# Groups of x: who centres and rounds them ahead of the transposes, and in which slot

## What is computed

```python
def _layernorm(x, axis=-1, eps=1e-05):
    m = jnp.mean(x, axis=axis, keepdims=True)
    v = jnp.var(x, axis=axis, keepdims=True)
    return (x - m) / jnp.sqrt(v + eps)

def _act_quant(x):
    scale = 127.0 / jnp.clip(jnp.max(jnp.abs(x), axis=-1, keepdims=True), 1e-05)
    xq = jnp.clip(jnp.round(x * scale), -128.0, 127.0) / scale
    return x + jax.lax.stop_gradient(xq - x)

x = x + jnp.tanh(g_xattn[0]) * _L0_xattn_ref(_layernorm(x), ctx_1024, ctx_1024, ...)
x = x + jnp.tanh(g_ffn[0]) * _L0_ffn_ref(_layernorm(x), w_gate, w_up, w_down)

gate = jax.nn.silu(_bitlinear(x, w_gate)); up = _bitlinear(x, w_up)
return _bitlinear(gate * up, w_down)        # each _bitlinear quantises its input with _act_quant
```

## Time and profile before

| | |
|---|---|
| median of three runs | 793.21 us (792.26 to 796.49) |
| the profiled execution | 792.8 us, of it the span from first to last instruction 791.0 us |
| busy share of the span | PE 89%, DVE 90%, ACT 86%, Pool 62% |
| slots 258 to 283 (groups 0 to 11) | about 641 to 688 us |
| tiles from s = 0 on | about 688 to 791 us |

### The profile page before, as it was taken

How to read it: one execution, slowest core, us unless ns; L and a number is a source line. 1 busy time by engine, 2 the same in 40 slices (tenths; PEclk the granted TensorE clock), 3 DMA queues, 4 the chain that set the end, 5 groups by cost and what they waited for, 6 DMA issues and landing times.

```text
span 791.0 us, 20866 instructions
## 1 busy us (share of the span) xinstructions
PE 702.7 (89%) x7118; PEld 474.6 (60%) x7127; DVE 708.0 (90%) x1452; ACT 683.9 (86%) x1454; POOL 487.9 (62%) x956
## 2 busy tenths in 40 slices
PE   6567899999999999999999999999999888877896
PEld 4334566666666666667676766676765555533453
DVE  5779899989899999999999999899999776798995
ACT  1578899898999999999999999999999888768883
POOL 4747657667777667676766666767664043245663
PEclk9666899999999999999999999999999899999998
DMA  9997747464668575767455666656664122246688
GB/s 206 204 261 166 197 127 149 109 126 128 154 120 149 124 144 124 145 122 158 123 138 134 134 137 133 128 136 130 124 118 85 39 68 86 71 103 164 160 179 181
DMA packets 148887, 108.50 MB, mean 137 GB/s; under 512 B 56991, under 2 KB 145183, under 8 KB 148767
## 3 DMA queue, kind: packets, MB, share of 16 engines
q1 hardware_dynamic: 143630, 101.98, 58.3%
q10 hardware_dynamic: 5152, 5.19, 2.7%
HBM read 49.54 MB, written 12.85 MB: 79 GB/s over the span
## 4 chain that ended last, share of the span: by engine, by line
PE 36%; ACT 35%; DVE 16%; issue 9%; DMA 2%; ACTq 1%; POOL 1%; SPq 0%; DVEq 0%; POOLq 0%
ACT ex L1197 13%; ACT pt L1187 12%; PE p_o L1348 7%; PE p_m L1426 6%; PE p_s L1328 5%; PE p_m L1407 5%; PE p_t L1369 4%; DVE kst L1032 3%; DVE hmax L1035 3%; PE p_m L1415 3%; ACT L1223 3%; ACT L1187 2%; DVE stats L907 2%; PE p_m L1399 2%; DVE nm L926 2%
## 5 line engine op out<-in xcount | busy, mean ns | idle before, releaser
L1197 ACT ACTIVATE ex<-p_s,nm 112x375 f32<-112x375 f32 x512 | 275.8, 618 | 12.3 <-DVE nm L926 11.0
L1187 ACT ACTIVATE pt<-p_t,ct 128x336 f32<-128x336 f32 x488 | 245.8, 577 | 26.7 <-PE p_t L1369 24.5
L907 DVE BATCH_NORM_STATS2 stats<-ex 112x6 f32<-112x375 f32 x512 | 252.5, 535 | 1.4 <-ACT ex L1197 1.3
L926 DVE TENSOR_REDUCE nm<-p_s 112x2 f32<-112x750 f32 x256 | 236.0, 922 | 1.2 <-PE p_s L1328 1.0
L1328 PE MATMUL p_s<-kst,qst 96*112 96x375 bf16 x512 | 154.8, 348 | 13.5 <-ACT ex L1197 7.3
L1369 PE MATMUL p_t<-qst,kst 99*128 99x112 bf16 x1464 | 115.1, 213 | 4.9 <-ACT pt L1187 4.0
L1369 PEld LDWEIGHTS p_t<-qst,kst 99*128 99x128 bf16 x1464 | 91.1, 98 | 44.0 <-issue 19.7
L1407 PE MATMUL p_m<-wv_sb,ctxt 128*128 128x256 f32 (+1 forms) x384 | 106.7, 401 | 4.7 <-DVE va L859 2.9
L1348 PE MATMUL p_o<-pt,va 128*32 128x112 f32 (+1 forms) x3072 | 101.7, 265 | 1.4 <-ACT pt L1187 0.8
L1426 PE MATMUL p_m<-ctxt,wk_sb 128*128 128x375 f32 x240 | 94.6, 518 | 1.7 <-DVE qf L875 1.1
L1328 PEld LDWEIGHTS p_s<-kst,qst 96*112 96x112 bf16 x512 | 67.0, 139 | 45.7 <-ACT ex L1197 34.6
(11 more groups left out here) (187 smaller groups left out, 1164.3 us busy)
## 6 DMA issues: line engine op xcount, KB each, us to landing
kst<-kp SPq DMA_DIRECT2D x378, 93.8 KB, 3.5
ctxt<-ctxt_dram SPq DMA_DIRECT2D x32, 375.0 KB, 4.2
qbounce<-qp SPq DMA_DIRECT2D x32, 168.0 KB, 2.5
qst<-qbounce SPq DMA_DIRECT2D x32, 168.0 KB, 3.6
qst<-qbounce SPq DMA_DIRECT2D x32, 112.0 KB, 3.4
xm<-x_dram SPq DMA_DIRECT2D x32, 112.0 KB, 2.4
x_dram<-x SPq DMA_DIRECT2D x32, 112.0 KB, 1.9
xt<-x_dram SPq DMA_DIRECT2D x28, 128.0 KB, 3.2
```

The source lines that it names most:

```text
L907: last = nc.vector.bn_stats(stats[:, nb % RING, 2 * pb + i], ex[0:SQ, 2 * (t % 2) + i, :])
L926: nc.vector.tensor_reduce(nm[:, n % RING, 2 * p:2 * p + 2], p_s[t % 2][0:SQ, :, 0:SK], axis=AX.X, op=ALU.max, negate=True).then_inc(s_max, 1)
L1187: nc.scalar.activation(pt[:, (2 * r + i) % 8], st_home(r, i)[:, 0:KC * SQ].rearrange("k (c q) -> k c q", c=KC), ACT.Exp, scale=ct[:, nr % ...
L1197: nc.scalar.activation(ex[0:SQ, 2 * ((t - 1) % 2) + i, :], p_s[(t - 1) % 2][0:SQ, i, 0:SK], ACT.Exp, bias=nm[:, ne % RING, h:h + 1]).then_ ...
```

## The change

Pool centres the groups and rounds them; ACT's `round_group` is gone, and with it the column of zeros. At slot 258 + 2i Pool negates the means of group i into `xneg` (the tile of the inverses, under another name), adds them to x in two instructions and signals `s_cen`. DVE takes maximum, scale and inverse one slot later, at 259 + 2i. Pool's `quant_group` stays at 260 + 2i and now first multiplies by the inverse and adds ROUND, in two instructions; in Pool's queue it stands ahead of the centring of the next group in the same slot. Loads wait for `s_cen` of the group two before. For groups 12 and 13 all steps behind the centring are a tile later; for groups 0 to 11 transposes and copies stay in their slots. The diff, without the counts of semaphores that follow from it:

```diff
@@ def load_group(i) (SyncE) @@
                 if i >= 2:
-                    sp.wait_ge(s_gx, count(4, i - 2, 1))
+                    sp.wait_ge(s_cen, count(1, i - 2, 1))
@@ slot(t) (Pool) @@
                 i = group_at(t, 2)
                 if i is not None:
                     quant_group(i)
+                i = group_at(t, 0)
+                if i is not None:
+                    centre_group(i)
+
+            def centre_group(i):
+
+                of = slice(GROUP * i, GROUP * (i + 1))
+                pool.wait_ge(s_ag, GROUP * (i + 1))
+                nc.gpsimd.tensor_scalar(xneg[:, of], mv2[:, of, 0], -1.0, 0.0, ALU.mult, ALU.add).then_inc(s_neg, 1)
+                pool.wait_ge(s_gl[i % 2], ring_count(16 * GROUP, i, 2))
+                if i == 0:
+                    pool.wait_ge(s_bn, SLOTS * B)
+                if i >= 2:
+                    pool.wait_ge(s_gq, count(1, i - 2, 1))
+                pool.wait_ge(s_neg, count(1, i, 1))
+                for g in range(GROUP):
+                    k = GROUP * i + g
+                    last = nc.gpsimd.tensor_scalar(fxn[:, i % 2, g], xl[:, i % 2, g], xneg[:, k:k + 1], 1.0, ALU.add, ALU.mult)
+                last.then_inc(s_cen, 1)
 
             def quant_group(i):
 
+                pool.wait_ge(s_gx, count(3, i, 3))
+                for g in range(GROUP):
+                    k = GROUP * i + g
+                    last = nc.gpsimd.tensor_scalar(fxn[:, i % 2, g], fxn[:, i % 2, g], xinv[:, k:k + 1], ROUND, ALU.mult, ALU.add)
+                last.then_inc(s_gr, 1)
                 pool.wait_ge(s_gr, count(1, i, 1))
@@ tile(s) (Pool) @@
-                if s - 2 in LATE_AT:
-                    quant_group(LATE_AT[s - 2])
+                if s - 3 in LATE_AT:
+                    quant_group(LATE_AT[s - 3])
+                if s in LATE_AT:
+                    centre_group(LATE_AT[s])
@@ slot(t) (DVE) @@
-                i = group_at(t, 0)
+                i = group_at(t, 1)
                 if i is not None:
                     x_group(i)
@@ x_group(i) (DVE) @@
-                dve.wait_ge(s_gl[i % 2], ring_count(16 * GROUP, i, 2))
-                dve.wait_ge(s_ag, GROUP * (i + 1))
-                if i == 0:
-                    dve.wait_ge(s_bn, SLOTS * B)
-                if i == TAILED:
-                    dve.wait_ge(s_e2, 2 * SLOTS * B)
-                    nc.vector.memset(zero, 0.0).then_inc(s_zero, 1)
-                    dve.wait_ge(s_zero, 1)
-                if i >= 2:
-                    dve.wait_ge(s_gq, count(1, i - 2, 1))
-                for g in range(GROUP):
-                    k = GROUP * i + g
-                    if i < TAILED:
-                        last = nc.vector.tensor_scalar(fxn[:, i % 2, g], xl[:, i % 2, g], mv2[:, k, 0:1], None, ALU.subtract)
-                    else:
-                        last = nc.vector.scalar_tensor_tensor(out=fxn[:, i % 2, g], in0=xl[:, i % 2, g], scalar=mv2[:, k, 0:1],
-                                                              in1=zero.to_broadcast([P, D]), op0=ALU.subtract, op1=ALU.add)
-                last.then_inc(s_gx, 1)
-                dve.wait_ge(s_gx, count(4, i, 1))
+                dve.wait_ge(s_cen, count(1, i, 1))
                 nc.vector.tensor_reduce(xmax[:, of], fxn[:, i % 2], axis=AX.X, op=ALU.max, apply_absolute_value=True).then_inc(s_gx, 1)
@@ slot(t) and tile(s) (ACT) @@
-                i = group_at(t, 1)
-                if i is not None:
-                    round_group(i)
-
-            def round_group(i):
-
-                act.wait_ge(s_gx, count(4, i, 4))
-                for g in range(GROUP):
-                    k = GROUP * i + g
-                    last = nc.scalar.activation(fxn[:, i % 2, g], fxn[:, i % 2, g], ACT.Copy, scale=xinv[:, k:k + 1], bias=ROUND)
-                last.then_inc(s_gr, 1)
```

More of the change, by code:

```diff
@@ L144, in gated_block @@
         xmax, xsc, xinv = sb("xmax", [P, TILES]), sb("xsc", [P, TILES]), sb("xinv", [P, TILES])
+        xneg = xinv
         gsc, usc = sb("gsc", [P, TILES]), sb("usc", [P, TILES])
@@ L214, in gated_block @@
         tail_ride = p_s[0][:, 1, 0:C * SQ].rearrange("p (c q) -> p c q", c=C)
-        zero = p_t[0][:, 511:512]
         p_g, p_u = p_s[0], p_s[1]
@@ L263, in gated_block @@
         s_sc0, s_raw, s_raw2, s_smallw = sem("s_f_scaled_by_pool"), sem("s_f_unclipped"), sem("s_f_unclipped_by_pool"), sem("s_setup_weights")
-        s_zero = sem("s_zero_column")
+        s_neg, s_cen = sem("s_f_means_negated"), sem("s_f_x_centred")
         s_bn2, s_ln2, s_sq2 = sem("s_f_bn"), sem("s_f_ln"), sem("s_f_sqrt")
@@ L967, in rows_scale @@
                 dve.wait_ge(s_ln2, count(3, j, 2))
-                dve.wait_ge(s_gx, count(4, end // GROUP))
+                dve.wait_ge(s_gx, count(3, end // GROUP))
                 nc.vector.tensor_tensor(rstd2[:, first:end], rstd2[:, first:end], xsc[:, first:end], ALU.mult).then_inc(s_ln2, 1)
@@ L976, in x_group @@
                 of = slice(GROUP * i, GROUP * (i + 1))
[L977 to L995 removed]
+                dve.wait_ge(s_cen, count(1, i, 1))
                 nc.vector.tensor_reduce(xmax[:, of], fxn[:, i % 2], axis=AX.X, op=ALU.max, apply_absolute_value=True).then_inc(s_gx, 1)
[L997 removed]
+                dve.wait_ge(s_gx, count(3, i, 1))
                 nc.vector.tensor_scalar(xsc[:, of], xmax[:, of], XSC_MIN, 1.0 / 127.0, ALU.max, ALU.mult).then_inc(s_gx, 1)
[L999 removed]
+                dve.wait_ge(s_gx, count(3, i, 2))
                 nc.vector.reciprocal(xinv[:, of], xsc[:, of]).then_inc(s_gx, 1)
@@ L1022, in tile @@
                     rows_scale(EARLY_TILES, TILES, 1)
-                if s - 5 in LATE_AT:
-                    copy_group(LATE_AT[s - 5])
+                if s - 6 in LATE_AT:
+                    copy_group(LATE_AT[s - 6])
                 n = s
@@ L1042, in tile @@
                         nc.vector.reciprocal(hinv[:, first:end], hsc[:, first:end]).then_inc(s_hinv, 1)
-                if s in LATE_AT:
-                    x_group(LATE_AT[s])
+                if s - 1 in LATE_AT:
+                    x_group(LATE_AT[s - 1])
                 n = s - Y_LAG - 1
@@ L1257, in tile @@
                         nc.scalar.activation(hr[n % HRING][:, half], hh[n % HHRING][:, half], ACT.Copy, scale=hinv[:, n:n + 1], bias=ROUND).then_inc(s_hr, 1)
-                if s - 1 in LATE_AT:
-                    round_group(LATE_AT[s - 1])
                 if s == SQ_AT:
@@ L1530, in tile @@
                         nc.tensor.matmul(p_u[:, 0, :], identb[:, :], wq8[0][:, 0:512], start=True, stop=True)
-                if s - 4 in LATE_AT:
-                    if LATE_AT[s - 4] == TAILED:
+                if s - 5 in LATE_AT:
+                    if LATE_AT[s - 5] == TAILED:
                         pe.wait_ge(s_otc, B)
-                    transpose_group(LATE_AT[s - 4])
+                    transpose_group(LATE_AT[s - 5])
             timeline(slot, tile)
```

2 lines of the change are left out of this document (removed).

## The result

| | before | after |
|---|---|---|
| median of four runs each, taken in turn | 793.17 us (792.26 to 796.49) | 801.12 us (800.34 to 804.73) |
| ratio | | 1.0109, interval 1.0065 to 1.0153 |
| the profiled execution | 792.8 us, span 791.0 | 800.34 us, span 798.5 |

The changed kernel is slower by 1.1%. Four milestones cut the profiled executions into stretches. The last of the features' instructions on Pool opens the stretch of the groups; tile 0's first product on TensorE ends it. Then come DVE's first product of the tiles and the last inverse of a tile.

A forecast was written before the change was run, and what follows sets the result against it. Hand-over length between engines, not load, bounds the groups; DVE bounds the tiles. Tile 0 starting 7.3 us later less 1.9 in the tiles gives +5.4 on 792.8: 798.2 us, range 792.5 to 817.

The forecast's parts named there:

- The forecast case: Whole kernel: Pool and DVE alternate without overlapping groups; 798.2 us, own range 792 to 802, chance 0.64.
- The prices on Pool: Pool's instructions per group: negation 0.20 us, each centring 0.48, each rounding 0.48, constant 0.62.
- The rival of the slow pair: Pool's centring: the addition and multiplication takes 1.23 us each, making the cycle 5.57 and the kernel 815; chance 0.27.
- The cycle: Early groups: one round of Pool and DVE work with all waits takes 4.07 us a group, against 3.63 before.
- The stretch of the groups: Twelve groups ahead of tile 0: cycles plus extra delays make tile 0 start 7.3 us later.
- the late row of attention and the guards: Early groups: the attention row, over 2 us late, adds 0.9 us; Pool's guards, three times 0.36, add 1.1 together.
- The slot of the features: Slot 260: Pool waits for DVE's L901 and makes two feature products before rounding, adding 1.3 us.
- The clock: TensorE: a granted clock falling in longer waits would make the forecast wrong; no term in the sum.
- The tiles: Feed-forward tiles: DVE, the bound there, loses the zeros and the centrings of groups 12 and 13, gaining 1.9 us.
- The small scalings beside Pool: DVE's small scaling: guards and L631 beside the levels would lengthen it six times by up to 0.6 us.
- The end: Stretch after the last inverse of a tile: no term in the forecast sum.
- The rival "not slower": Early groups: with a cycle under 3.4 us, ACT's and DVE's relief shows, 786.5 us; decided at 3.63; chance 0.09.

The follow-up runs named there:

- e1: Changed kernel with Pool's two calls swapped, so Pool centres group i before it rounds group i-1: 793.04 us, 0.9990 of before.
- e9: Changed kernel without negated means, Pool's centring subtracting the mean instead of adding its negative: 813.35 us, 1.0224 of before.
- e6: Changed kernel with unread products on TensorE in the 22 slots in which the groups run: 800.49 us, 1.0077 of before.
- e2: Kernel before with only late groups 12 and 13 centred and rounded by Pool: 791.14 us, 0.9957 of before.
- e10: Kernel before with groups 12 and 13 rounded by Pool, not ACT, and still centred by DVE: 0.9998 of before.
- e5: Changed kernel with the means of group i+1 negated right behind the centring of group i: 796.53 us, 1.0021 of before.
- e8: Changed kernel with both the edit of e1 and that of e5: 792.24 us, 0.9973 of before.
- e3: Changed kernel with only early groups 0 to 11 on Pool, groups 12 and 13 as before: 802.75 us, 1.0103 of before.
- e12: e11 with six output buffers in place of four: median 790.13 us, 0.9934 of before.
- e7: Changed kernel, but groups 0 to 11 centred by DVE as before and rounded by Pool: 788.47 us, 0.9929 of before.
- e11: e7 with a few of e6's unread TensorE products in the last eight slots ahead of tile 0: 0.9925 of before.

## Why the prediction was right, and where it was off

Forecast 798.2 us, range 792.5 to 817, slower by over 0.5% 0.65; measured 801.12. The forecast case came true, by its mechanism: e1 brings the kernel level with before by order alone. The total came nearer than its parts. In the groups and at tile 0 the sum was 4.6 us too small (10.22 + 1.71 against 7.3), and 2.7 us that the start and the end gave back, where the forecast had nothing and no run ties them to the change, hide more than half of it. That is luck. By the prediction's own steps:

- **The prices on Pool** held: centring 0.477 (0.48), rounding 0.478 (0.48), negation 0.192 (0.20), DVE's levels 1.10 (1.09). The rival of the slow pair fell, and e9 shows why: it hangs on the subtraction.
- **The cycle** was 4.15, not 4.07. The term that was too small is Pool's wait for its own negation: 0.20 in place of 0.09, twelve times, 1.3 us. The row it was read from, 0.08 between two features of 32 columns, was not of this kind; why this one is longer no run shows. DVE's wait for Pool was 0.03 in place of 0.09; with spans of 0.94 where 0.92 stood, centring and wait together took 0.97 in place of 1.01.
- **The stretch of the groups** was +10.2, not +7.3. Of the 2.9 missing, 0.9 are the cycles (11 x 0.08), 0.2 the start of group 0, and about 1.5 the extras: the late row of attention and the guards came to 3.5 in place of 2.0. The value product of slot 262 ran at half clock, 2.07 for 1.09, so group 3 came 2.1 us late, where 0.9 and one guard's 0.36 stood, and the later guards stuck out 0.61 and not 0.36. The slot of the features was right (1.19 for 1.3). The end of the stretch took 0.5 more, for attention's last output stands ahead of the transposes, it waited for a DVE copy behind the levels of group 11, and it ran at half clock: constant off at 695.94, transposes at 696.46.
- **The clock** was named as what could make the sum wrong and stood in it with nothing. It cost 1.7 at tile 0; e6 gives 1.4 of that back. The trace of before could have priced it: one product of L1407 takes 0.379 us there at the median and up to 0.778, one of L1415 0.379 and up to 0.769. That the clock could fall ahead of tile 0 wasn't in that profile, which has 1.00 from 640 us on; e2 and e10 show that it also happens with the early groups of before.
- **The tiles** gained 1.74, forecast 1.9. But that was partly luck: in six experiments with the late groups on Pool (e1, e2, e5 to e8) the stretch takes 86.4 us, 2.6 less than before, and 3.6 to 3.8 less than in e3 and e10, which keep DVE's centring. Part of the missing 0.7 is DVE's small scalings held by Pool: in the kernel before they took 0.30 and 0.76 for groups 12 and 13 (the latter is the maximum of the earlier trace rows), in e2 0.17 and 0.57, which is 0.3 less. The other 0.4 stays open. The profiled execution of after lost 0.9 of it again, to windows with a clock of 0.94 and 0.92.
- **The small scalings beside Pool** were expected to be held six times. None of the twelve was: L1006 took 0.17 each time. In nine of them Pool waits or has just ended L631; in the three beside the guards L1006 starts within 0.1 us of the end of L685 and is through at about the start of L689. The upper edge of the forecast case had counted these six at half of the 0.6 named for each: 1.8 + 1.9 = 3.7; at the full 0.6 it would have been 5.5. The rule itself holds in the kernel before, in DVE's and Pool's timelines:

```profile
682.62 0.70 DVE L998 TENSOR_SCALAR xsc<-xmax 128x2 f32<-128x2 f32 x1
```

```profile
682.57 0.73 POOL L631 TENSOR_TENSOR xm<-xm,bo_sb 112x256 f32<-112x256 f32 x1
```

  682.62 + 0.70 is 683.32, and Pool's instruction ends at 683.30. The Trainium skill, SBUF — State Buffer, section Who interferes with whom, says that between a DVE instruction in a two-port mode and a GpSimd one whoever issues first holds the shared ports for its whole instruction; the trace agrees.
- **The end** was taken as unchanged and was 1.78 shorter: DVE's waits there for output transfers to free a buffer were 4.6 us before and 1.6 after. e12 shows that such waits can be taken away, and that another transfer is then late. How much of the 1.78 is the change's doing and how much differs from run to run stays open; so does the 0.91 ahead of the features, where the change does nothing.
- **The rival "not slower"** needed a cycle under 3.63 us. It was 4.15, and e5 shows how near it was: without the negation on the ring it is 3.76, and the kernel is level with before, with the gain of the tiles counted in.

## What to carry to other kernels

When work moves to an engine with room, look at what stands ahead of it in that engine's queue: if that waits for something that the moved work must first release, two stages run in turn, and the pace is the sum of all hand-overs, whatever the loads are. Here swapping two calls was worth 1.2%, and taking one instruction of two columns, and the wait for it, off the ring 0.9%. What gained against before was to move the centring only where its old engine is full (e2), with or without the early rounding, a step that closes no circle (e7).

## What was new about the hardware

- Pool's tensor_scalar of 256 columns takes 0.48 us as add and multiply or multiply and add with one value of the partition, and 1.14 us as subtract and multiply (e9, with the reservation made there). The Trainium skill, GPSIMD Engine Reference, section Engine selection, calls one-input work there roughly line-rate; here it depends on the pair of operations.
- Pool waits 0.20 us for a result of its own of two columns, and 0.08 us in the row of before; DVE waits 0.03 us for Pool.
- TensorE's granted clock read 0.50 from 684 to 700 us in the changed kernel, where it waited 1.42 and 1.76 us for Pool. But it read 0.52 to 0.63 from 684 to 692 us in e2 and e10 too, after no wait over 1.0 us from 676 us on in e2, and 1.00 in the profile of before, whose instructions and spacing there are the same. With unused products in the slots it was 1.00 from 660 us on (e6) or throughout the groups (e11). What decides it between two executions of the same work no run shows. A clock of 1.00 was worth 1.4 us at tile 0 (e6) and 3.0 us over e7's groups (e11's profile); e11's median is no better than e7's.
